# A DLRM tower kernel: layer 0 in six full tiles and a stacked half tile, and one more group split with its low part on GpSimd

## What is computed

```python
x0 = xk = e                                   # (B, 39, 16)
for idx, W in enumerate((w0, w1, w2)):        # W: (39, fields of xk, 128)
    z = relu(einsum('bhd,bkd,hks->bsd', x0, xk, W) + b)
    # layers 0, 1: xk = z[:, :64], z[:, 64:] goes to the logit; layer 2: all of z does
logit = sum(concatenate(direct, axis=1), axis=-1)
```

## Time and profile before

| | |
|---|---|
| median of 3 runs | 667.73 us (666.85 to 668.83) |
| the profiled execution | 668.06 us, its span 666.2 us |
| PE, DVE, POOL, ACT busy | 625.0, 576.7, 463.1, 283.8 us |
| one chunk | 37.1 us |

### The profile page before, as it was taken

How to read it: one execution, slowest core, us unless ns; L and a number is a source line. 1 busy time by engine, 2 the same in 40 slices (tenths; PEclk the granted TensorE clock), 3 DMA queues, 4 the chain that set the end, 5 groups by cost and what they waited for, 6 DMA issues and landing times.

```text
span 666.2 us, 7143 instructions
## 1 busy us (share of the span) xinstructions
PE 625.0 (94%) x1916; PEld 357.9 (54%) x1916; DVE 576.7 (87%) x507; ACT 283.8 (43%) x341; POOL 463.1 (70%) x277
## 2 busy tenths in 40 slices
PE   0358999999999999999999999999999999999998
PEld 0124555565555555555655555555655555555553
DVE  3139899999999999999999999999999999999670
ACT  3014444534454444444444444445444544445223
POOL 5607678686987878786978878786868878716340
PEclk9997999999999999999999999999999999999999
DMA  6698787694949495785939395876949395862000
GB/s 226 149 214 185 158 198 149 148 202 105 217 94 221 81 221 115 178 171 130 215 82 220 77 225 102 196 153 145 202 98 217 81 218 104 199 131 67 1 1 0
DMA packets 27422, 98.19 MB, mean 147 GB/s; under 512 B 7377, under 2 KB 16337, under 8 KB 18962
## 3 DMA queue, kind: packets, MB, share of 16 engines
q1 hardware_dynamic: 20930, 94.05, 63.9%
q0 software_dynamic: 5120, 1.32, 2.0%
q10 hardware_dynamic: 1360, 2.69, 1.1%
HBM read 94.20 MB, written 3.84 MB: 147 GB/s over the span
## 4 chain that ended last, share of the span: by engine, by line
PE 81%; DVE 6%; issue 3%; ACT 2%; POOL 1%; DVEq 0%; ACTq 0%; POOLq 0%
PE z L516 37%; PE z L527 12%; PE z L522 12%; PE z L524 11%; DVE products L404 5%; PE z L507 4%; PE z L510 2%; POOL low L280 1%; PE z L509 1%; PE spare L560 1%; ACT high L625 1%; PE z L584 1%; DVE low L280 1%; PE xk L584 1%; ACT xk L609 0%
## 5 line engine op out<-in xcount | busy, mean ns | idle before, releaser
L404 DVE TENSOR_TENSOR products<-x_rep,xk 128x1024 f32<-128x1024 f32 (+1 forms) x288 | 366.7, 1333 | 29.1 <-ACT xk L609 19.8
L280 POOL TENSOR_TENSOR low<-products,high 128x1024 fp32r<-128x1024 f32 x112 | 264.9, 2390 | 131.5 <-ACT high L625 90.0
L516 PE MATMUL z<-products,w_whole 128*128 128x512 f32 x672 | 312.9, 598 | 0.0
L625 ACT ACTIVATE high<-products 128x1024 fp32r<-128x1024 f32 x176 | 184.3, 1056 | 242.1 <-DVE products L404 200.1
L360 POOL DMA_INDIRECT gathered<-in_tables,rows_sb x160 | 197.5, 1234 | 46.5 <-issue 44.6
L522 PE MATMUL z<-high,w_high 128*128 128x512 f32 x352 | 188.0, 534 | 15.8 <-ACT high L625 15.8
L516 PEld LDWEIGHTS z<-products,w_whole 128*128 128x128 f32 x672 | 128.5, 191 | 112.8 <-issue 98.0
L524 PE MATMUL z<-high,w_low 128*128 128x512 f32 x352 | 139.7, 397 | 0.0
L527 PE MATMUL z<-low,w_high 128*128 128x512 f32 x352 | 113.9, 404 | 3.7 <-DVE low L280 2.9
L522 PEld LDWEIGHTS z<-high,w_high 128*128 128x128 f32 x352 | 66.9, 190 | 61.6 <-issue 33.2
L280 DVE TENSOR_TENSOR low<-products,high 128x1024 fp32r<-128x1024 f32 x64 | 93.8, 1467 | 1.3 <-ACT high L625 1.3
(11 more groups left out here) (34 smaller groups left out, 102.5 us busy)
## 6 DMA issues: line engine op xcount, KB each, us to landing
x_rep<-x_rows SPq DMA_DIRECT2D x64, 768.0 KB, 16.7
x_rep<-x_rows SPq DMA_DIRECT2D x64, 512.0 KB, 9.3
x_rows<-gathered SPq DMA_DIRECT2D x16, 225.0 KB
x_rep<-in_w ACTq DMA_DIRECT2D x2, 1280.0 KB, 9.9
gathered<-in_tables,rows_sb POOLq DMA_INDIRECT x160
x_same<-x_rows SPq DMA_DIRECT2D x16, 90.0 KB
x_same<-x_rows SPq DMA_DIRECT2D x16, 78.0 KB
x_rep<-in_wt SPq DMA_DIRECT2D x2, 512.0 KB, 4.0
```

Of the source, the lines that this page charges most:

```text
L280: ops.tensor_tensor(low[0:p, slot, 0:n, :], products[0:p, index % RING, 0:n, :], high[0:p, slot, 0:n, :].bitcast(fp32), ALU.subtract).then ...
L404: nc.vector.tensor_tensor(slots, rep, row.unsqueeze(1).broadcast_to([p, n, N]), ALU.mult).then_inc(made, 1 + pair)
L516: mm = nc.tensor.matmul(out, w_whole[0:p, at, i, :], products[0:p, slot, i, :], start=(t + i == 0), stop=(t + i == tiles[layer] - 1))
L625: nc.scalar.activation(high[0:p, slot, 0:n, :], products[0:p, index % RING, 0:n, :], ACT.Copy).then_inc(rounded, 1)
```

## The change

Layer 0's pairs are laid out anew (`ANCHORS`, `row_of`): the upper 64 partitions take their replicated rows from a start that is turned by 5, so that all pairs fit in six full tiles and one of 64 partitions. That half tile is a new kind of group, `s` (`ALONE`): ACT rounds it, DVE makes its low part into `stacks`, and PE takes it with the two matmuls of L509 and L510, without a whole tile before them. It comes third in layer 0. `x0_same` is now loaded with six DMAs a chunk and not four, of the same bytes in all; the replicated rows keep their parts and sizes.

The letters change: layer 1 `pwppwpwddh` -> `wppwppwddh` (as many of each letter as before), layer 0 `dwww` -> `wdsd`, layer 2 `wdwpwpwpwh` -> `wwpwpwpwph`. A chunk has then 20 whole tiles (23 before), 12 split groups (11), of them 8 with the low part on POOL (7) and 4 on DVE (4), and 3 stacks (2). Since a group need no longer start with tile 0, waits, `start` and `stop` of the matmuls go by the group's index. `logits2` moves from after group 8 to after group 6, `after_layer1` from before group 12 to before group 14, `after_layer0` from before group 18 to before group 19.

```diff
-ANCHORS = [(0, F, 0), (F, HALF - F, F - 2 * T0), (HALF, 19, 6), (HALF + 19, 45, 32)]
+TURNED = 5
+ANCHORS = [(0, 34, 12), (34, 30, 14), (HALF, 9, 5), (73, 6, 6), (79, F, 1), (118, 10, 31)]
+def row_of(e, t):
+    return T1 + (t + TURNED) % (T1 - 1) if e else t
 def field_of(p, t):
-    return (p % HALF + p // HALF * T1 + t) % F
+    return (p % HALF + row_of(p // HALF, t)) % F
...
+def parts_new(index):
+    layer, t, n = BODY[index][:3]
+    tiles = range(t, t + n)
+    before = {part_of(u) for i in range(STARTS[layer], index) for u in range(BODY[i][1], BODY[i][1] + BODY[i][2])}
+    return sorted({part_of(u) for u in tiles} - before)
...
-LETTER = {"w": WHOLE, "d": LOW_DVE, "p": LOW_POOL, "h": STACKED}
-KINDS = {1: "pwppwpwddh", 0: "dwww", 2: "wdwpwpwpwh"}
+ALONE = "one tile of 64 partitions, split and stacked"
+LETTER = {"w": WHOLE, "d": LOW_DVE, "p": LOW_POOL, "h": STACKED, "s": ALONE}
+KINDS = {1: "wppwppwddh", 0: "wdsd", 2: "wwpwpwpwph"}
...
     for letter in KINDS[layer]:
+        if letter == "s":
+            found.append((layer, tiles - 1, 1, partitions[-1:], ALONE))
+            tiles -= 1
+            continue
...
-L0_GROUPS = groups_of(0, T0, [S] * T0)
+L0_GROUPS = groups_of(0, T0, [S] * (T0 - 1) + [HALF])
...
-                    src = x0_rows[bass.ds(c, 1), T1 * e + first:T1 * e + first + 1, :]
+                    src = x0_rows[bass.ds(c, 1), row_of(e, first):row_of(e, first) + 1, :]
...
-                    if kind in (LOW_DVE, STACKED):
+                    if kind in (LOW_DVE, STACKED, ALONE):
                         late.append(index)
...
-                    if index == 8 and not (isinstance(c, int) and c == 0):
+                    if index == 6 and not (isinstance(c, int) and c == 0):
                         logits2(c - 1)
...
-                if kind == STACKED:
-                    at, stack = WHOLES.index(index), STACKS.index(index)
-                    pe.wait_ge(made, count("all", c, index))
-                    nc.tensor.matmul(out, w_whole[:, at, 0, :], products[:, slot, 0, :], start=False, stop=False)
+                if kind in (STACKED, ALONE):
+                    stack = STACKS.index(index)
+                    if kind == STACKED:
+                        pe.wait_ge(made, count("all", c, index))
+                        nc.tensor.matmul(out, w_whole[:, WHOLES.index(index), 0, :], products[:, slot, 0, :],
+                                         start=False, stop=False)
                     pe.wait_ge(stack_low, count("stacked", c, index))
-                    nc.tensor.matmul(out, w_stack_high[:, stack, :], stacks[:, stack, :], start=False, stop=False)
+                    nc.tensor.matmul(out, w_stack_high[:, stack, :], stacks[:, stack, :], start=first, stop=False)
                     mm = nc.tensor.matmul(out, w_stack_low[:, stack, :], stacks[0:HALF, stack, :],
-                                          start=False, stop=True)
+                                          start=False, stop=last)
...
-                    if index == N1 + 2:
+                    if index == N1 + 4:
                         after_layer1(c)
-                    if index == N1 + N0 + 4 and not last:
+                    if index == N1 + N0 + 5 and not last:
                         after_layer0(c)
```

More of the change, by code:

```diff
@@ L45, in pairs_of_layer0 @@
     for t in range(T0):
-        for p in range(S):
+        for p in range(S if t < T0 - 1 else HALF):
             pair = frozenset((anchor_of(p), field_of(p, t)))
@@ L53 @@
 PARTS = [(0, 4), (4, 8), (8, 14), (14, T1)]
+assert all(row_of(1, end - 1) - row_of(1, first) == end - 1 - first for first, end in PARTS)
 def part_of(t):
     return next(q for q, (first, end) in enumerate(PARTS) if first <= t < end)
+def parts_new(index):
[3 more added lines that the diff above has]
+    return sorted({part_of(u) for u in tiles} - before)
 DENSE = 16
@@ L93 @@
 SPLIT = [i for i, g in enumerate(BODY) if g[4] in (LOW_DVE, LOW_POOL)]
-STACKS = [i for i, g in enumerate(BODY) if g[4] == STACKED]
+STACKS = [i for i, g in enumerate(BODY) if g[4] in (STACKED, ALONE)]
+STARTS = {1: 0, 0: N1, 2: N1 + N0}
+ENDS = {1: N1 - 1, 0: N1 + N0 - 1, 2: len(BODY) - 1}
 RING = 8
@@ L109 @@
     "split": lambda g: g[4] in (LOW_DVE, LOW_POOL),
-    "stacked": lambda g: g[4] == STACKED,
+    "stacked": lambda g: g[4] in (STACKED, ALONE),
     LOW_DVE: lambda g: g[4] == LOW_DVE,
@@ L327, in _ @@
             load_same(1, 1)
-            sp.wait_ge(w_copied, len(BODY))
+            sp.wait_ge(w_copied, len(WHOLES) + len(SPLIT))
             sp.wait_ge(w_stack_made, len(STACKS))
@@ L422, in make_low @@
                     at = STACKS.index(index)
-                    nc.vector.tensor_tensor(stacks[HALF:128, at, :], products[0:HALF, index % RING, 1, :],
+                    nc.vector.tensor_tensor(stacks[HALF:128, at, :], products[0:HALF, index % RING, BODY[index][2] - 1, :],
                                             stacks[0:HALF, at, :].bitcast(fp32), ALU.subtract).then_inc(stack_low, 1)
@@ L432, in body @@
                     if layer == 1:
-                        if t == 0:
+                        if index == STARTS[1]:
                             dve.wait_ge(xk0_ready, c + 1)
-                        if t == PARTS[part_of(t)][0]:
-                            dve.wait_ge(rep_loaded[part_of(t)], 32 * (c + 1))
+                        for q in parts_new(index):
+                            dve.wait_ge(rep_loaded[q], 32 * (c + 1))
                     if layer == 0:
-                        if t == 0:
+                        if index == STARTS[0]:
                             dve.wait_ge(same_loaded, 16 * len(ANCHORS) * (c + 2))
-                        if t == PARTS[part_of(t)][0]:
-                            dve.wait_ge(rep_loaded[part_of(t)], 32 * (c + 2))
-                    if layer == 2 and t == 0:
+                        for q in parts_new(index):
+                            dve.wait_ge(rep_loaded[q], 32 * (c + 2))
+                    if index == STARTS[2]:
                         while late:
@@ L476, in _ @@
                                           w_sb[layer][0:p, t:t + n, :]).then_inc(w_copied, 1)
-                else:
+                elif index in SPLIT:
                     at = SPLIT.index(index)
@@ L486, in _ @@
                 dve.wait_ge(w_stack_rounded, at + 1)
-                nc.vector.tensor_tensor(w_stack_low[:, at, :], w_sb[layer][0:HALF, t + 1, :],
+                nc.vector.tensor_tensor(w_stack_low[:, at, :], w_sb[layer][0:HALF, t + BODY[index][2] - 1, :],
                                         w_stack_high[0:HALF, at, :].bitcast(fp32), ALU.subtract) \
@@ L498, in _ @@
         def _(pe):
-            tiles = [T0, T1, T1]
             def contract(c, index):
@@ L503, in contract @@
                 slot, out = index % RING, z[layer][:, :]
-                if kind == STACKED:
-                    at, stack = WHOLES.index(index), STACKS.index(index)
-                    pe.wait_ge(made, count("all", c, index))
-                    nc.tensor.matmul(out, w_whole[:, at, 0, :], products[:, slot, 0, :], start=False, stop=False)
+                first, last = index == STARTS[layer], index == ENDS[layer]
+                if kind in (STACKED, ALONE):
[4 more added lines that the diff above has]
+                                         start=False, stop=False)
                     pe.wait_ge(stack_low, count("stacked", c, index))
-                    nc.tensor.matmul(out, w_stack_high[:, stack, :], stacks[:, stack, :], start=False, stop=False)
+                    nc.tensor.matmul(out, w_stack_high[:, stack, :], stacks[:, stack, :], start=first, stop=False)
                     mm = nc.tensor.matmul(out, w_stack_low[:, stack, :], stacks[0:HALF, stack, :],
-                                          start=False, stop=True)
+                                          start=False, stop=last)
                 elif kind == WHOLE:
@@ L516, in contract @@
                         mm = nc.tensor.matmul(out, w_whole[0:p, at, i, :], products[0:p, slot, i, :],
-                                              start=(t + i == 0), stop=(t + i == tiles[layer] - 1))
+                                              start=(first and i == 0), stop=(last and i == n - 1))
                 else:
@@ L522, in contract @@
                         nc.tensor.matmul(out, w_high[0:p, at, i, :], high[0:p, part, i, :],
-                                         start=(t + i == 0), stop=False)
+                                         start=(first and i == 0), stop=False)
                         nc.tensor.matmul(out, w_low[0:p, at, i, :], high[0:p, part, i, :], start=False, stop=False)
@@ L527, in contract @@
                         mm = nc.tensor.matmul(out, w_high[0:p, at, i, :], low[0:p, part, i, :],
-                                              start=False, stop=(t + i == tiles[layer] - 1))
+                                              start=False, stop=(last and i == n - 1))
                 mm.then_inc(used, 1)
```

(21 more changed lines are left out.)

## The result

The changed kernel takes 708.02 us (706.56 to 708.85), before 668.19 (the median of four runs now): a ratio of 1.059 (1.058 to 1.061). The forecast was 657, the range ended at 687, and the rival that came true, POOL in DVE's way, had been priced at 690, outside that range.

The account below looks back on a forecast made before the run. PE was taken as the bound, only just ahead of DVE, with POOL's part deciding. Fourteen periods at 36.6 for 37.14 gave -7.6, the ends the rest: -10.4 us in all, so 657 us (-1.6%), range 652 to 687.

Parts of the forecast that it names:

- POOL in DVE's way: Rival at DVE's last stack of the chunk: it waits for POOL's fourth low part; 38.9 a period, 690 us; chance 0.22.
- POOL's part: Layer 2's four POOL low parts: DVE asks at M + 35.6, enters after the third; period 36.6 instead of 37.14.
- the gathers: POOL's ten gathers a chunk, each waiting for the end of the DVE instruction it meets: +0.3 us for the ten.
- the 38.9 of the text: Upper bound of the period: POOL keeps SBUF for its fourth low part in layer 2, 38.3 + 0.6 us.
- The second rival: Gathers come a whole step earlier, so the fourth low part hits DVE's stack: period 37.8 to 38.0, 675 us; chance 0.12.
- PE's prices: PE's work: whole tile 0.86, split group 1.39, stack 0.85 us; the change saves 0.34 a chunk, leaving 36.4.
- DVE's order: DVE's times after layer 1's first product pair (M): layer 2 at M + 22.9, SBUF request at M + 35.6, no xk1 wait.
- Chunk 14, without gathers: POOL's last low part starts just ahead of DVE and ends at M + 37.4: period 38.0, +0.8 us.
- The start: First round: PE's remaining layer 0 takes some 4.5 us for 6.62 (-2.2), DMAs +0.6; together -1.6 us.
- The two more DMAs: Two extra loads for x0_same ahead of the replicated rows in the first round, 0.33 us each: +0.6 us.
- Chunk 0: First chunk, 38.8 us, 1.7 above a steady one: PE starts 1.2 us earlier with a whole group first, -1.3 us.
- The last chunk: Layer 1's stalls and PE's lag go, PE's work from there on is the same: -0.7 us.

Follow-up runs that it names:

- e9: Kernel before with twelve split groups on old layer 0, no paired products, and a gate (POOL's fourth layer-2 low part waits for DVE's stack): 655.2 us, ratio 0.983.
- e2: Kernel before with only layer 2's letters changed, wdwpwpwpwh to wwpwpwpwph, on the old layout: 661.5 us, ratio 0.991.
- e8: Kernel before with twelve split groups on the old layer 0 (ddww), layer 2 wwpwpwpwph, no paired products, no gate on POOL: 667.9 us, ratio 1.000.
- e7: e2 with a shorter reduction after group 18, summing only 2 of each 16 numbers: 680.3 us, ratio 1.016 to the kernel before.
- e6: Changed kernel with the half tile's group last in layer 0 (wdds for wdsd): 696.6 us, ratio 1.041 to the kernel before.

## Why the prediction was wrong

- **The failed step** is the one at POOL's part: "If DVE is let in when it ends, the next pair comes 0.58 after the end of POOL's (422.76 - 422.18), at M + 36.6. This is my value for the period". DVE is not let in. It asks at 443.61, during the third low part, and goes on behind the fourth, which begins only at 445.06. I took the gathers as the nearest rows. They show POOL getting in between two of DVE's instructions, and I turned that round without a row for it. The whole slower side hung on this choice; I gave its opposite 0.22. With the wait for all four at the forecast times the period would have been the 38.9 of the text, and the time its 690: the step alone puts the time beyond the range, whose end of 687 was set below the price of a case with that chance.
- **A term that was mis-sized**: the gathers, "+0.3 for the ten", measured +1.6 (14.3 for 12.7); behind them PE waits 2.04 for group 16's low part, where 0.3 was forecast. The fourth isn't served at the end of the DVE instruction it meets but two later. This makes 38.9 into 40.1, and with it 690 into 708. The second rival had gathers a step *earlier*; none had them later.
- **Right**: PE's prices. A stack between two split groups costs 0.87 (0.33 + 0.43 + 0.11) for 0.85, so the half tile saves PE nothing, and the period of a PE-bound kernel with this count is 36.34 for 36.4 (e9). DVE's order was right within 0.1: layer 2 at M + 23.0, no wait for xk1, the request at M + 35.7. Chunk 14, without gathers, was near too: 38.4 for 38.0.
- **The start** gained 3.2 and not 1.6. The rest of layer 0 takes PE the 4.5 us of the text, but I set it against the 6.62 of the whole tiles alone and left out the split group's own last matmuls ahead of them (1.0). The two more DMAs, put at +0.6, cost nothing. **Chunk 0** took 40.55 for 38.82. Its surplus over a steady chunk fell from 1.7 to 0.4, the 1.3 of the text, but by luck: POOL closes this chunk like the others, its stack waiting 3.11, and PE's earlier start has no part in it. **The last chunk** and what follows it took 0.95 more where 0.7 less was forecast; its stack asks while POOL's last low part has 1.98 to run and lasts 2.52.
- **On the rule for the shared pair**: the Trainium skill ("SBUF — State Buffer", section "Who interferes with whom") also says that issue order decides who blocks. In the trace DVE's stack asked 1.45 us before POOL's fourth low part began and still came after it. That low part was ready in POOL's queue, though, from 442.88 on, when ACT had rounded its input, 0.73 before DVE asked; which of the two orders counts the runs don't tell. The gathers are held up beside two-input instructions (mostly 1.3 to 3.3 us, 0.94 beside one-input ones), against what its sentence that a tensor_tensor does not hold up descriptor generation would let one expect; but a gather also reads its row numbers from SBUF (`rows_sb`), and no run separates that read from the descriptors.

## What to carry to other kernels

When two engines share a port, look not only at whether they collide but at what is queued behind the holder: a run of instructions on one engine can hold the other for all of them, and an added wait that breaks the run can be worth more than work taken away (here 28 us). Where the trace lacks the decisive case, its mirror image isn't evidence; the price must be carried at both ends and the chance kept near even. Moving work to the engine with idle time pays only if that engine's new place in time is free, too: e9 and the change have the same counts of split groups and of low parts on POOL and DVE, but for the half tile's, and differ by 53 us (by the gate, the pairs, layer 1's order and the layout of layer 0).

## What was unexpected of the hardware

- With another low part ready behind the one that runs, DVE's stack goes in at once when it asks 0.20 us before the end (e2), and waits for both when it asks 0.43 before (3.3 us, e8), 1.1 (4.0, e7) or 1.5 (4.4, changed). Between, time alone doesn't decide: it is let in at 0.30, 0.29 and 0.24 (e7, chunks 0, 1 and 14), and waits 3.1 at 0.24 (changed kernel, chunk 0). What else decides isn't settled by these runs.
- A gather that is issued 0.12 us before DVE goes on from its half product to the next instruction takes 3.30, with 1.56 where it meets a full product. Why it misses two of DVE's ends, and why another in e6 misses one, isn't settled by these runs.
